# One more wait in front of the convolution's matrices, in an eight-layer model on one Trainium2 core

## The reference

```
x = x + tanh(g_xattn[0]) * cross_attention_16_heads(layernorm(x), ctx)
x = x + tanh(g_ffn[0])   * top1_routed_experts(layernorm(x))          # 8 experts
x = x + tanh(g_xattn[1]) * topk_attention_film_s4d(layernorm(x), ctx) # the layer that convolves
x = x + tanh(g_ffn[1])   * soft_mixture(layernorm(x))
x = x + tanh(g_xattn[2]) * cross_attention_8_heads(...)
...
```

```
y[b, l, d] = sum_{s <= l} K[d, l - s] * x[b, s, d] + D_skip[d] * x[b, l, d]
```

## Time and profile before

| | |
|---|---|
| median of 3 runs | 1509.52 us (1508.18 to 1509.85) |
| the profiled execution, its own time | 1522.08 us |
| span of its instructions | 1520.4 us |
| busy: PE, DVE, ACT, POOL | 88%, 72%, 61%, 45% of the span |
| chain that ended last | PE 60%, DVE 18%, issue 8%, ACT 6%, POOL 5%, DMA 2% |
| mean granted TensorE clock | 0.942 |
| DMA packets, bytes | 66868, 43.05 MB, mean 28 GB/s |

### The profile page before, as it was taken

How to read it: one execution, slowest core, us unless ns; L and a number is a source line. 1 busy time by engine, 2 the same in 40 slices (tenths; PEclk the granted TensorE clock), 3 DMA queues, 4 the chain that set the end, 5 groups by cost and what they waited for, 6 DMA issues and landing times.

```text
span 1520.4 us, 49785 instructions
## 1 busy us (share of the span) xinstructions
PE 1343.0 (88%) x17625; PEld 1029.3 (68%) x17657; DVE 1090.0 (72%) x4573; ACT 922.1 (61%) x2012; POOL 687.8 (45%) x1336
## 2 busy tenths in 40 slices
PE   6999999999658688887789599988999999999998
PEld 5888888877545344444556366666877777788885
DVE  5878788877424799999868544436899899766664
ACT  5666665655335577787233355545688889865553
POOL 3655555576434688766166211113443343343331
PEclk9999999999875888899989799998999999999999
DMA  8050000001455401000020100000000000000000
GB/s 186 3 123 0 0 0 2 5 29 34 124 168 134 96 18 29 1 0 1 16 52 0 36 1 0 0 1 2 3 2 0 0 2 3 3 9 7 7 15 22
DMA packets 66868, 43.05 MB, mean 28 GB/s; under 512 B 24597, under 2 KB 63210, under 8 KB 66602
## 3 DMA queue, kind: packets, MB, share of 16 engines
q1 hardware_dynamic: 58346, 33.89, 9.1%
q0 software_dynamic: 2048, 4.20, 1.0%
q10 hardware_dynamic: 6336, 3.15, 0.7%
HBM read 28.64 MB, written 12.58 MB: 27 GB/s over the span
## 4 chain that ended last, share of the span: by engine, by line
PE 60%; DVE 18%; issue 8%; ACT 6%; POOL 5%; DMA 2%; DVEq 1%; SPq 0%; POOLq 0%; ACTq 0%
PE ps L775 4%; PE ps L344 4%; PE ps L784 4%; DVE arena L1992 4%; PE ps L386 4%; PE ps L337 4%; PE ps L366 3%; PE ps L2723 3%; DVE arena L1986 3%; PE ps L2730 3%; PE ps L377 3%; PE ps L2804 3%; PE ps L357 2%; PE ps L2717 2%; PE ps L2773 2%
## 5 line engine op out<-in xcount | busy, mean ns | idle before, releaser
L3236 POOL TENSOR_TENSOR arena<-arena 128x512 f32<-128x512 f32 x64 | 67.8, 1059 | 112.6 <-DVE arena L3160 112.6
L1992 DVE MATCH_REPLACE8 arena<-arena 128x64 f32<-128x64 f32 x512 | 101.8, 209 | 0.5 <-issue 0.2
L2482 DVE TENSOR_SCALAR_CACHE_REDUCE thr_hits<-thr_abs,thr_candidate 128x512 bf16<-128x512 f32 (+1 forms) x248 | 101.8, 477 | 0.0
L2723 PE MATMUL ps<-arena,toeplitz 96*128 96x128 f32 x512 | 71.5, 283 | 9.2 <-ACT arena L2955 4.0
L668 POOL TENSOR_TENSOR ln_veps<-ln_mv,eps 128x4 f32<-128x4 f32 x32 | 9.1, 284 | 154.5 <-DVE ln_mv L662 154.5
L1986 DVE MAX8 arena<-arena 128x8 f32<-128x64 f32 x512 | 75.9, 210 | 3.3 <-issue 2.0
L616 POOL TENSOR_TENSOR arena<-arena 128x1024 f32<-128x1024 f32 x32 | 61.4, 1918 | 34.8 <-DVE arena L557 34.8
L538 DVE TENSOR_REDUCE arena<-ps 128x16 f32<-128x1024 f32 x32 | 39.1, 1223 | 52.9 <-PE ps L357 52.8
L784 PEld LDWEIGHTS ps<-arena,toeplitz 128*128 128x128 f32 x512 | 63.5, 192 | 16.0 <-issue 13.3
L386 PEld LDWEIGHTS ps<-arena 128*64 128x64 f32 x1024 | 60.2, 139 | 19.8 <-issue 11.4
L2723 PEld LDWEIGHTS ps<-arena,toeplitz 96*128 96x128 f32 x512 | 63.0, 193 | 15.0 <-ACT arena L2955 9.8
(11 more groups left out here) (463 smaller groups left out, 4157.2 us busy)
## 6 DMA issues: line engine op xcount, KB each, us to landing
toeplitz<-ssm_toeplitz_scratch SPq DMA_DIRECT2D x2, 2048.0 KB
arena<-L_ffn_packed SPq DMA_DIRECT2D x24, 128.5 KB, 3.2
toeplitz<-L_ffn_packed SPq DMA_DIRECT2D x24, 128.5 KB, 2.2
f_rows<-arena SPq DMA_DIRECT2D x2, 1536.0 KB, 9.5
f_outs<-arena ACTq DMA_DIRECT2D x12, 256.0 KB, 2.7
ssm_toeplitz_scratch<-ssm_padded_kernel SPq DMA_DIRECT2D x1, 2048.0 KB
out<-x_res SPq DMA_DIRECT2D x8, 256.0 KB, 2.3
arena<-ctx SPq DMA_DIRECT2D x2, 768.0 KB, 5.8
```

The lines of the kernel that those rows point to most:

```text
L1992: ins = V.match_replace(W2[:, s, h, :], m8[:, r, h, :], src[:, s, h, :], TAKEN)
L2482: ins = V.tensor_scalar(self.hits[:, j, at:at + n], self.abs[:, at:at + n], self.cand[:, c:c + 1].bitcast(F32), 0.0, ALU.is_ge, ALU.add, a ...
L2723: last = T_.matmul(ps[:, 0, c * P:(c + 1) * P], weights[phase].k[0:DC, c * P:(c + 1) * P], cg[0:DC, s, :], start=True, stop=True)
L3236: G_.tensor_tensor(probs, probs, rc[:, s, :].unsqueeze(2).to_broadcast([P, heads, CTX]), ALU.mult).then_inc(s_prob.sem, 1)
```

## The change

SP waits for one more semaphore in front of the matrices' write: `x_done` of the routed layer at its end value, 32, that is for DVE to have taken the last gathered tile. Nothing else differs.

```diff
     def sp_matrices(self, e):
         e.wait_ge(self.summed.sem, 3)
         e.wait_ge(self.toep_free.sem, self.toep_free.end)
+        e.wait_ge(self.rows_taken.sem, self.rows_taken.end)
 
         windows = self.padded[:, self.L - 1:2 * self.L - 1]
@@
         route.loaded = loaded
-        k.ssm.toep_free = route.o_full
+        k.ssm.toep_free, k.ssm.rows_taken = route.o_full, route.x_done
         new()
```

## The result

Before: 1510.84 us, median of 17 runs. After: 1500.89 us, median of 17 runs on the same chip. The medians differ by 9.95 us; the ratio estimated from all runs is 0.9939 [0.9923, 0.9956] (in brackets the 95% interval), that is 0.61% or some 9.2 us faster. Forecast were 0.63% and 1500.0 us.

A forecast was written before the change was run, and what follows sets the result against it. It took PE to be in most of the chain, but DVE's gather waits and POOL's pace to bound the changed stage. Terms -9.57 + 0 + 0 + 0 took 1509.52 to 1499.95, say 1500.0 us; range 1497.5 to 1506.5.

The forecast's parts named there:

- The gathers were held up by the fetch, and the waits go: DVE steps 2 and 3: gathers of pairs 0 and 1 are late beside the matrices' fetch; moving it removes both waits.
- Sizes of the waits: DVE's waits for the gathers at the start of steps 2 and 3: 7.51 and 2.84 us, both to go.
- POOL caps the gain: POOL sets the pace from pair 3 to pair 12, so only its stalls of 6.36 and 3.21 us count: 9.57 us.
- The DVE count: DVE alone in steps 2 and 3 would gain 7.51 + 2.84 + 1.10 = 11.45 us.
- FiLM has 0.8 us to spare: Step 2: ACT lays the film at 503.5, POOL reaches it at 504.27, 0.8 us later, so no wait.
- Moved transfers and SP's later loads cost nothing: Behind the last take: matrices lie by 629, wanted at 732.65; sublayer 4's loads have 94 us of cover; cost 0.
- The profiled time: Whole profiled execution: 1522.08 us before would become 1512.5 us.
- carry the whole difference over: Whole kernel: the profiled gain of 9.57 us applies in full to the unprofiled median, 1509.52 us.
- ACT cutting the gain: Rival: film late in steps 2 and 3, only 6.36 us won, 1503.2 us, said as 1503; chance 0.14.
- DVE's gain in full: Rival: DVE, not POOL, sets the pace behind step 4, so 11.45 us come, 1498.1 us; chance 0.08.
- Another reason for slow gathers: Rival: DVE's work holds up the gathers, pairs 0 and 1 stay slow, time stays 1509.5 us; chance 0.08.
- The slower one: Rival: DVE's or POOL's loop starts inside the moved fetch and stalls up to 14.74 us, 1514.7 us; chance 0.08.

The follow-up runs named there:

- the light pair: Before and after, each with four POOL operations per step on 8 of 128 columns; step 0's end to last take 111.37 and 100.08 us.
- the moved and the paced fetch: After with the write waiting only for pair 1: 1520.13 us; before with sixteen 256 KB fetches, only the last two open: 1512.12 us.
- twice the traffic: After with each matrix fetched twice, one pair of DMAs behind the other: 1504.89 us in one execution.

## Why the prediction was right

*The gathers were held up by the fetch, and the waits go.* Right. The waits left DVE's steps 2 and 3, and a fetch put elsewhere among the gathers brought them back. The forecast took "bytes" for the cause, which is only part of it: the same bytes in short runs with at most 512 KB open cost nothing. I had not separated them.

*Sizes of the waits.* Right as a sum, by luck in its parts. A second profile of the same kernel, with pair 0 issued ahead of the fetch, had 0 and 11.22 us for 7.51 and 2.84.

*POOL caps the gain.* Right. The forecast's 6.36 + 3.21 = 9.57 met 9.75 to 9.87. The DVE count, 11.45, met 11.29 as soon as POOL was made light. Of all steps this one carried most: without it I would have said 1498.1. The first take that waits for POOL's pace is that of step 7 in after, for a forecast of step 6.

*FiLM has 0.8 us to spare.* The sign held: after has no wait at L1834 in steps 2 to 4.

*Moved transfers and SP's later loads cost nothing.* Right in effect. The write took 589.76 - 578.40 = 11.36 us, the fetch ended some 22 us after its issue, and the convolution began at

```profile
718.04 4.18 PE L2363 MATMUL ps<-arena,toeplitz 64*64 64x32 f32 x137
```

which is 734.0 on before's clock. The forecast had 732.65. In the first pair of traces 1.48 us were lost behind the last take. The repeats of after have 138.50 and 138.53 us there, for 138.25 and 137.63 of before, and the light pair has no difference. So the zero was up to 0.9 us too small by the repeats, and at most 2.1, which the runs cannot resolve. One thing was missed: SP itself stood 15.12 us at two small loads of sublayer 4 behind the fetch, where it took 0.96 us for them before. DVE first works on sublayer 4's weights at L2538, so this stayed hidden:

```profile
709.33 0.70 DVE L2538 TENSOR_SCALAR arena<-thr_abs,thr_found 128x512 f32<-128x512 f32 x1
```

*The profiled time.* I put the changed kernel's profile at 1512.5 us; it was 1497.95. The step "carry the whole difference over" held for the medians and failed for the single execution, since before's had 15.9 us more ahead of the stage, by nothing that the change does.

*The rivals.* ACT cutting the gain: no wait for the film. DVE's gain in full: only with a light POOL. Another reason for slow gathers: refuted by after, where steps 2 and 3 have no wait with DVE busy 21.46 of 22 us, and by the moved and the paced fetch. The forecast's own argument against it, a DMA share of 0.97, was weak: that was the fetch's traffic, and it does not tell whether a gather's descriptors came late. The slower one, a stall at a loop's entry beside the fetch: DVE's largest idle time there was 0.42 us, and twice the traffic brought no stall.

What stays open: how the loss comes about inside the DMA engines, with the backlog and the load of the engines not told apart, and what stops PE and DVE for 0, some 6 or some 13 us near 415 us in some executions. POOL is not stopped there: in before it issues DMAs for 9.20 of the 13 us from 414 to 427. This stop is seen with and without the change, and no run looked for its cause.

## What to carry to other kernels

Before a large prefetch is put "where there is room", look which small transfers with a waiting reader share the engines, and either start it behind the last of them or send it in short runs with only little of it open at a time (512 KB here); both recovered the same 9.8 us. Then price the gain by the slowest engine that follows: DVE's waits came to 11.3 us, and POOL, which paces the loop behind them, let 9.8 through. Compare traces by the stretch between two instructions that both kernels have, since the spans differed by 24.2 us for a change of 9.8.

## What the hardware did that I had not expected

A gather of 64 KB needs 2.53 to 2.58 us alone. Beside two transfers of 2048 KB that had been queued whole it took 16.21 us and its reader stood 11.22 us; beside the same bytes cut into sixteen with 4 KB runs but queued at once, 8.27 and 3.56 us; and with only two of the sixteen open its reader stood at most 0.6 us, the usual wait of these steps.

The Trainium skill, DMA: Bandwidth & Descriptors, section Queues, rings and completion order, has each engine take turns between its queues packet by packet. By that a gather should wait for about a packet at each of its turns and not for the backlog, and shorter packets should have been nearly enough. The trace agrees in part: short runs gave back 6.4 of 9.8 us. The other 3.4 us came back when fewer bytes were open and the engines less loaded, which that rule alone does not give.

An engine that issues DMAs can be held up by them: SP issued sixteen transfers of 256 KB in 10.19 us, 0.64 us each, but in after stood for 15.12 us at two small ones behind the 4.19 MB of the fetch, for 0.96 us at the same two in before.

TensorE's clock was lower where it stood: in the same steps the granted clock was 0.73 with PE busy 14.94 of 22 us, and 0.91 with 17.99. The two levels are 1.2 and 2.4 GHz, and these are means over them.
